# A two-layer graph network on one core: padded bias rows, a re-cut setup, 64-node spans and four groups moved to the second layer

## The reference

```
# layer 0 (row = src, col = dst)
deg   = segment_sum(w, row);  dinv = rsqrt(deg)           # with self loops of weight 1
out   = segment_sum(dinv[row] * w * dinv[col] * (h @ kernel)[col], row)
x     = x + relu(out + bias)
# layer 1 (heads = src, tails = dst; E = edge_attr_128)
fwd   = concat(H[heads], E) @ W_fwd  + b_fwd              # summed at tails
back  = concat(H[tails], E) @ W_back + b_back             # summed at heads
agg   = segment_sum(messages) / (count + 1e-7)
x     = x + gamma * layernorm(leaky_relu(agg) + H) + beta
```

## Time and profile before

| | us |
|---|---|
| median of 3 runs (4246.0 to 4250.3) | 4246.62 |
| profiled execution, its own time | 4252.24 |
| its span, first to last instruction | 4250.4 |
| mean granted clock of PE | 0.915 of full |
| busy: PE / DVE / POOL / ACT | 3448.3 / 3101.1 / 3055.5 / 1865.2 |

### The profile page before, as it was taken

The page is one execution under the profiler, slowest core; times in us unless marked ns, Lnnn a source line. Parts: engine busy times, 40 slices in busy tenths (PEclk is TensorE's granted clock), DMA queues, the critical chain, the costliest instruction groups (busy, mean ns, idle before and its releaser), DMA issues. The chain is left out here.

```text
span 4250.4 us, 99711 instructions
## 1 busy us (share of the span) xinstructions
PE 3448.3 (81%) x30414; PEld 2895.6 (68%) x30630; DVE 3101.1 (73%) x7790; ACT 1865.2 (44%) x4527; POOL 3055.5 (72%) x1813
## 2 busy tenths in 40 slices
PE   3455699888889889889834789898989898898987
PEld 3344687777777777777724677777777677777666
DVE  8799888888888888888726766666766676666423
ACT  1020455555555555555424344444444444444523
POOL 4778688888888888888841888777877787787210
PEclk8788899999999999999966799999999999999965
DMA  9992787777777777777777555444544455454931
GB/s 174 272 234 16 157 144 143 139 136 141 136 143 143 134 142 138 136 145 135 141 145 204 82 84 81 79 78 80 85 79 78 78 80 81 77 83 70 132 100 31
DMA packets 731785, 505.05 MB, mean 119 GB/s; under 512 B 306293, under 2 KB 643226, under 8 KB 731236
## 3 DMA queue, kind: packets, MB, share of 16 engines
q0 software_dynamic: 257584, 176.81, 37.0%
q1 hardware_dynamic: 473528, 321.32, 29.1%
q10 hardware_dynamic: 124, 0.05, 0.0%
HBM read 284.18 MB, written 240.17 MB: 123 GB/s over the span
## 5 line engine op out<-in xcount | busy, mean ns | idle before, releaser
L827 POOL DMA_INDIRECT gcn_sums<-fl_sums,fl_to_i x864 | 1439.4, 1666 | 293.6 <-DMA gcn_sums<-fl_sums,fl_to_i 155.0
L1686 POOL DMA_INDIRECT gcn_sums<-shared,ds_to_i x752 | 1293.9, 1721 | 466.4 <-ACT shared L1937 245.1
L1892 PE MATMUL bank<-ds_counts,ds_parts 128*128 128x256 bf16 x3675 | 606.8, 278 | 0.0
L1961 ACT COPY ds_turned<-bank 128x1024 bf16<-128x1024 bf16 (+1 forms) x325 | 313.2, 964 | 598.4 <-PE bank L1877 467.9
L1055 ACT COPY fl_sums<-bank 128x256 f32<-128x256 f32 x864 | 325.3, 377 | 552.7 <-PE bank L983 342.2
L1925 ACT CAST ds_counts<-bank 128x392 bf16<-128x392 f32 x800 | 382.6, 491 | 219.9 <-PE bank L1836 191.9
L865 DVE SCALAR_TENSOR_TENSOR fl_same<-fl_key_b,fl_pat,bank 128x128 f32<-128x128 bf16 x864 | 372.7, 443 | 113.9 <-PE bank L983 91.1
L1912 PE MATMUL bank<-ds_turned,ds_now 128*128 128x512 bf16 (+1 forms) x1734 | 420.7, 372 | 12.1 <-issue 0.9
L1854 PE MATMUL bank<-shared 128*128 128x128 f32 x1504 | 310.4, 311 | 118.3 <-DVE attr_sums L1738 89.7
L1821 DVE TENSOR_TENSOR src_sums<-src_sums,bank 128x512 f32<-128x512 f32 (+1 forms) x325 | 212.9, 655 | 261.7 <-PE bank L1912 257.4
L982 PE MATMUL bank<-fl_pay,fl_same 128*128 128x128 f32 x1728 | 348.5, 284 | 48.9 <-issue 34.7
(11 more groups left out here) (264 smaller groups left out, 7167.6 us busy)
## 6 DMA issues: line engine op xcount, KB each, us to landing
fl_attrs<-in_edge_attr SPq DMA_DIRECT2D x108, 512.0 KB
shared<-in_edge_attr SPq DMA_DIRECT2D x186, 256.0 KB
fl_rel_b<-dst_offset SPq DMA_DIRECT2D x108, 256.0 KB
fl_key_b<-src_key SPq DMA_DIRECT2D x108, 256.0 KB
gcn_sums<-zeros SPq DMA_DIRECT2D x40, 640.0 KB
shared<-src_key SPq DMA_DIRECT2D x94, 256.0 KB
gcn_sums<-fl_sums,fl_to_i POOLq DMA_INDIRECT x864
near<-src_float SPq DMA_DIRECT2D x1, 12892.0 KB
```

What stands on the lines that cost most here:

```text
L827: nc.gpsimd.indirect_dma_start(out=d.tab_gcn[j % K], out_offset=bass.IndirectOffsetOnAxis(ap=to_i[:, (GPI * kk + gi) % 4, j:j + 1], axis=0 ...
L1686: nc.gpsimd.indirect_dma_start(out=d.tab_gcn[j % K].rearrange("n (two f) -> (n two) f", two=2), out_offset=bass.IndirectOffsetOnAxis(ap=to ...
L1892: ins = nc.tensor.matmul(row_bank[:, 0:2 * P], parts[:, tile, s, :], counts[:, h, tile, :, :].rearrange("p b q -> p (b q)"), start=(tile = ...
```

## The change

Four edits.

1. *Last nodes.* The rows of counts and of biases get 128 partitions instead of 2; the other 126 are zero (a POOL memset of half the counts, two DVE memsets), ACT's DMAs of the two real rows wait for them, and the bias product comes last of the five.
2. *Setup.* One semaphore for each of dst, src, w; x is loaded after all stores; DVE starts on dst as soon as it is in; SP stores dst's copies and reads the heads back before the rest; the first set of one-hots comes after `search_heads` instead of ahead of it; the first section has one more pair and the last one fewer; the row one-hot is two instructions of 128x2048; one more maximum in `offsets` guards edit 3.
3. *Second layer.* Windows of W = 64 nodes instead of 128: L1729 compares with 0..63, the window matmuls have 64 moving columns, L1738 adds 64.
4. *Four groups.* G1 = 104, so the first layer's last slot has only products; NB = 98, BT = 23, so super-tile 22 has groups beside it and `between` comes after it.

```diff
-G1 = GPI * (2 * DS + 1)
+W = 64
+G1 = GPI * 2 * DS
-        SECTIONS = ((1, 7, "search_rows"), (7, 10, "offsets"), (10, 14, "search_edges"), (14, 16, "deviations"), (16, 21, "places"), (21, LAST // 2, None))
+        SECTIONS = ((1, 8, "search_rows"), (8, 11, "offsets"), (11, 15, "search_edges"), (15, 17, "deviations"), (17, 22, "places"), (22, LAST // 2, None))
...
-            load_x(sp, d, x, x_in)
-            sp.wait_ge(runs_ready, 5)
+            sp.wait_ge(runs_ready, 3)
             sp.dma_start(lines(d.dst_f), dst_run).then_inc(dst_stored, 16)
-            for a, t in ((d.samples, samples[:]), (d.dst_key, key16[:, 1, :]), (d.src_f, src_run), (d.w_f, w_run),
-                         (d.src_key, key16[:, 0, :]), (d.src_i, src_i), (d.dst_i, dst_i)):
+            for a, t in ((d.samples, samples[:]), (d.dst_key, key16[:, 1, :]), (d.dst_i, dst_i)):
                 sp.dma_start(lines(a), t).then_inc(runs_stored, 16)
             sp.wait_ge(dst_stored, 16)
             sp.dma_start(heads[:], ...)
             sp.dma_start(next_first[0:P - 1, :], ...)
+            sp.wait_ge(runs_ready, 5)
+            for a, t in ((d.src_f, src_run), (d.src_key, key16[:, 0, :]), (d.src_i, src_i)):
+                sp.dma_start(lines(a), t).then_inc(runs_stored, 16)
+            sp.wait_ge(w_in, 16 * 3)
+            sp.dma_start(lines(d.w_f), w_run).then_inc(runs_stored, 16)
+            load_x(sp, d, x, x_in)
...
-            dve.wait_ge(edges_in, 16 * 9)
+            dve.wait_ge(dst_in, 16 * 3)
...
+                nc.vector.tensor_reduce(wide[:, 3:4], rec[:, G1:, 2, :], mybir.AxisListType.XY, ALU.max)
...
-                nc.vector.tensor_tensor(in_twos(row_hot[:, h, 0:count, :]), counted(P), pair(row_of, P), ALU.is_equal)
+                for at in range(0, count, WJ):
+                    nc.vector.tensor_tensor(in_twos(row_hot[:, h, at:at + WJ, :]), counted(P, WJ), pair(row_of, P, at, WJ), ALU.is_equal)
...
-            one_hots(0, 0)
             check_order()
             search_heads()
+            one_hots(0, 0)
             one_hots(0, 1)
...
             def slot(i, kk, last):                    # first layer: SP, POOL, PE, ACT, DVE alike
-                for gi in range(GPI):
+                for gi in range(0 if last else GPI):
...
-            with eng.Fori(1, BT // 2 - 1) as i:       # second layer
+            with eng.Fori(1, BT // 2) as i:
                 pair_of_tiles(i, 0, True, False)
                 pair_of_tiles(i, 1, True, False)
-            pair_of_tiles(BT // 2 - 1, 0, True, False)
-            pair_of_tiles(BT // 2 - 1, 1, True, False)
+            pair_of_tiles(BT // 2, 0, True, False)
             if between:
                 between()
...
-            pair_of_tiles(SUPER // 2 - 1, 0, False, False)
-            pair_of_tiles(SUPER // 2 - 1, 1, False, False)
+            pair_of_tiles(BT // 2, 1, False, False)
             pair_of_tiles(SUPER // 2, 0, False, True)
...
-                nc.vector.tensor_tensor(sum_hot, d.iota[:].unsqueeze(1).to_broadcast([P, J, P]), rec[:, p, 2, :].unsqueeze(2).to_broadcast([P, J, P]),
+                nc.vector.tensor_tensor(sum_hot, d.iota[:, 0:W].unsqueeze(1).to_broadcast([P, J, W]), rec[:, p, 2, :].unsqueeze(2).to_broadcast([P, J, W]),
                                         ALU.is_equal).then_inc(sum_ready, 1)
...
-                    nc.tensor.matmul(win_bank[:, 0:P], attrs[:, jj // U, jj % U, :], sum_hot[:, jj, :], start=(jj == 0), stop=(jj == J - 1))
+                    nc.tensor.matmul(win_bank[:, 0:W], attrs[:, jj // U, jj % U, :], sum_hot[:, jj, :], start=(jj == 0), stop=(jj == J - 1))
...
-        count_rows = sb("count_rows", [2, ROWS])      # last nodes
-        bias_rows = sb("bias_rows", [2, F])
+        count_rows = sb("count_rows", [P, ROWS])
+        bias_rows = sb("bias_rows", [P, F])
+            nc.gpsimd.memset(count_rows[:, ROWS // 2:], 0.0).then_inc(rows_zeroed, 1)
...
+            nc.vector.memset(bias_rows[:], 0.0).then_inc(rows_zeroed, 1)
+            nc.vector.memset(count_rows[:, 0:ROWS // 2], 0.0).then_inc(rows_zeroed, 1)
...
-                if t == 0:
-                    pe.wait_ge(counts_in, 64)
-                nc.tensor.matmul(out, count_rows[:, t * NP:(t + 1) * NP], bias_rows[:], start=False, stop=False)
                 pe.wait_ge(turn_copied, t + 1)
                 nc.tensor.matmul(out, turn_sb[:, t % 2, :], w[:, 0, :], start=False, stop=False)
...
-                nc.tensor.matmul(out, row_sums[:, t * NP:(t + 1) * NP], w[:, 3, :], start=False, stop=True).then_inc(prod_ready, 1)
+                nc.tensor.matmul(out, row_sums[:, t * NP:(t + 1) * NP], w[:, 3, :], start=False, stop=False)
+                if t == 0:
+                    pe.wait_ge(counts_in, 64)
+                nc.tensor.matmul(out, count_rows[:, t * NP:(t + 1) * NP], bias_rows[:], start=False, stop=True).then_inc(prod_ready, 1)
...
+            act.wait_ge(rows_zeroed, 3)
```

57 lines of the change are left out of this document (31 added, 26 removed).

## The result

The changed kernel took 4145.32 us (median of 4 runs, 4135.06 to 4146.58); the kernel before, in the same rounds, 4246.31 (4237.49 to 4250.30). The ratio is 0.976, with a 95% interval of 0.9738 to 0.9781. Run again later beside other kernels it took 4136.25 us, ratio 0.9749 (0.9730 to 0.9767). The forecast was 4142. The profiled execution took 4146.58 us, its span 4144.8, so 105.6 us less than the 4250.4 of before; the sum of the forecast was 105. That agreement is partly luck: several terms were off by 2 to 7 us and one was missing, and they cancel.

What follows compares the result with a forecast made beforehand. It took chained DVE and POOL to bound setup, POOL the first layer, PE the second layer and last stage. Terms of -54, -15, -57, +20, +21 and -20 us sum to -105: median 4142, range 4090 to 4180.

Steps and rivals of the forecast that it cites:

- Edit 1: Last stage: equal row counts save 0.62 us a tile and let PE's clock rise; 93 us instead of 147, -54.
- The memsets "at nothing": Last stage: they delay ACT's DMAs by about 2 us beside the loads of gamma and beta, costing nothing.
- the cover that I named: Last stage: loads of gamma and beta hide the delay of ACT's DMAs; without them it costs the 2 us.
- Edit 2: Setup: first gather at about 44 instead of 55.5, less DVE idling, one pair fewer behind `places`; -15 us.
- Edit 4, first layer: End of first layer: 32 scatters fewer take 60 us off POOL's end, then the products end last; -57 us.
- Edit 4, second layer: Second layer's end: super-tile 22 with groups, +20 us; table loads no longer hidden, stage ends later, +21 us.
- Edit 3: Second layer: 29 PE waits for DVE's chain each 0.65 us shorter, -20 us; PE's matmuls gain nothing.
- (1): Last stage: the clock stays low, 116 instead of 93 us; 4167 us in all; chance 0.17.
- (2): Last stage: row count does not matter, so tile cost and clock stay as they are; 4196 us; chance 0.05.
- (3): Second layer: PE streams the halved columns faster, as far as POOL lets it; 4082 us; chance 0.12.
- (4): Second layer: PE, less busy, loses full clock in stretches, 0.87 instead of 0.97; +157, so 4300 us; chance 0.04.
- Rival 5: First layer's products end at 2140 or later and the table loads are slowed too; 4172 us; chance 0.07.

Runs made afterwards that it cites:

- undo_groups: Changed kernel with 108 groups in the first layer again and the last pair of tiles outside the loop; 4144.66 us, ratio 0.9757 to the kernel before.
- pair_out: Changed kernel with tiles 20 and 21 outside the second layer's loop again, groups left as changed; 4130.97 us, ratio 0.9740 to the kernel before.
- undo_span: Changed kernel with windows of 128 nodes again (W = 128) instead of 64; 4162.32 us, ratio 0.9801 to the kernel before.
- pe_full: Changed kernel with PE's window product at 128 moving columns again, DVE's comparison and addition staying at 64; 4126.78 us, ratio 0.9729 to the kernel before.
- after_again: The changed kernel run again, the same code; 4136.25 us, ratio 0.9749 to the kernel before.
- undo_bias: Changed kernel with two rows of counts and biases again, their product third of the five, no memsets; 4195.03 us, ratio 0.9876 to the kernel before.
- rows64: Changed kernel with the bias product over 64 of the 128 padded rows; 4154.77 us, ratio 0.9787 to the kernel before.

## Why the prediction was right, and where its steps failed

- **Edit 1** (-54): -55.7 measured, and the mechanism as put: two rows held the clock at 0.50, and the change of row count costs by itself. The memsets "at nothing" were not: the first tile's products end 14.5 us into the stage instead of 13.0, so the cover that I named was absent and 1.5 of the 2 us came out. The Trainium skill, TensorE: Matmul & The Clock Gate, section "What happens when you issue a matmul", says that a load's time goes with its columns and not with its rows. The loads in these traces agree, 0.29 us with 64 rows against 0.30 with 128. The prediction read this sentence too widely when it drew from it that padding saves nothing: it does not speak of a change of row count between neighbours, and that is what costs, 1.57 against 1.23 us a tile, both at full clock.
- **Edit 2** (-15): 14.5 us at the histogram, 10.9 at the first layer. The step that failed is what was not walked: with one pair of sets fewer behind `places`, POOL's memset falls on a DVE comparison that it stops for 3.6 us. I had followed POOL's gathers, not the instruction behind them. The Trainium skill, Trainium Architecture — The Big Picture, section "What this means for kernel authors", says that the ports that DVE and GpSimd share are held exclusively, not split; the 3.83 us instead of 0.19, ending with the memset, agree. Not every DVE instruction was held: a copy and three additions beside the same memset took their usual time.
- **Edit 4, first layer** (-57): -63.8 up to the nodes' PE. POOL's part was -62.6 against -60; the rest is that the products, costed to end at 2120 on the old clock, did end there (2108.9 + 10.9) and what follows waits less long.
- **Edit 4, second layer** (+20 and +21): +17.7 and +21.0. What the sum lacked is the loop. The diff moves the pair of tiles 20 and 21 from outside the loop into it, one more turn, and I costed that edit at nothing without naming it: 4.5 us in the trace of before against after; at equal spans 7.2 to 7.6 us with 64 nodes (undo_groups, pair_out) and 4.9 with 128 (undo_span against before). So edit 4 was not worth 16 us but about none in this kernel (undo_groups), and 28 without the turns.
- **Edit 3** (-20): 17 to 22 us by the ratios, 24 to 30 in the second layer's trace. The size was near, but the mechanism was only half of it: a wait costs PE not only its length but, often, half clock behind it, and behind the shorter wait that was rarer (9 of 23 against 18 of 23). That PE gains nothing from 64 columns was right.
- The **rivals**: the clock did rise (1), rows do matter (2), PE did not gain from columns (3), the second layer kept 0.97 (4). Rival 5 named the wrong place for edit 4's loss: the products and the loads came as forecast, the loop was dearer.

The misses cancel. Between the traces of before and after, edit 1 is 1.7 us better than forecast, setup 4.1 worse, the first layer 6.8 better, tile 22 2.3 better and the loads as forecast. What is left of the second layer, its prologue and the rest behind the nodes, where the spans and the loop act together, is -13.9 us (-3.1 - 14.8 + 4.5 - 0.5) instead of -20, 6.1 worse. The sum is 0.6 better.

**Open.** PE's stop at a turn differs from kernel to kernel. It was 2.2 to 2.3 us on average in before, undo_groups and undo_span (17.5 and 18.4 us in 8 stops, 21.1 in 9), 2.5 in pe_full (22.5 in 9), whose loop differs from the changed kernel's only by a product's width and a comparison's output, and 3.0 to 3.4 in the changed kernel, after_again, undo_bias and rows64 (30.5, 27.8, 29.2 and 26.7 in 9). Where the code lies may decide; no run tested that. It is also why differences of 5 to 10 us between kernels with loops are not safely an edit's. What holds the clock at 0.50 with a product of two rows and not with one of 64 is also open, and so is what two rows as the last of the five would do. A second memset of POOL (L845, 431.47, 5.43 us) lies over a DVE cast (L931) that takes 5.00 us in the changed kernel and 5.01 before (then L917); moving that one wasn't tried.

## What to carry to other kernels

A small operand can cost more than its work: a matmul of two rows beside four of 128 kept the whole stage at half clock, and zero rows were the cure. When groups of work are moved, follow every loop bound and every load that was hidden behind what moved; cost a loop's turn, here 7 to 8 us a time on the engine that bounds, and look whether writing it out is possible. A chain of accumulating loads, each waiting for the one before, leaves the DMA engines idle at every link; issued in two independent halves, one half's transfer ran while the other was issued.
